# Attention of a fused layer on Trainium2: channel vectors kept as columns, one product for the maxima, and the first inverse root moved between weight pieces

## The reference

```
qkv = x @ w_qkv.T ; q, k, v = thirds of qkv            # c = 256
agent = q @ w_conv1                                    # [b, n]
agent_attn = softmax((agent * c**-0.5) @ k)            # [b, c], over channels
agent_v = softmax(v @ agent_attn)                      # [b, n], over tokens
agent_v = agent_v @ v                                  # [b, c]
agent_tok = softmax(agent[:, :, None], axis=-1)
x = layernorm(x + agent_tok * agent_v[:, None, :])
x = layernorm(x + ffn(x))        # 8 experts, 2 per token, plus a shared gated layer
```

## Time and profile before

| | |
|---|---|
| median of 3 runs | 362.53 us (361.86 to 367.12) |
| profiled execution, time | 358.51 us |
| profiled execution, span of the trace | 356.7 us |
| PE busy | 319.7 us (90%) |
| PE weight loads busy | 284.6 us (80%) |
| DVE busy | 264.1 us (74%) |
| POOL busy | 205.3 us (58%) |
| ACT busy | 191.6 us (54%) |

### The profile page before, as it was taken

The page is one execution under the profiler, slowest core; times in us unless marked ns, Lnnn a source line. Parts: engine busy times, 40 slices in busy tenths (PEclk is TensorE's granted clock), DMA queues, the critical chain, the costliest instruction groups (busy, mean ns, idle before and its releaser), DMA issues.

```text
span 356.7 us, 7798 instructions
## 1 busy us (share of the span) xinstructions
PE 319.7 (90%) x2225; PEld 284.6 (80%) x2225; DVE 264.1 (74%) x1032; ACT 191.6 (54%) x424; POOL 205.3 (58%) x241
## 2 busy tenths in 40 slices
PE   3789899899999989997987999999999989989970
PEld 1356788589788878886967999999999989978860
DVE  1876779665989898964647677676678868787786
ACT  1043777355556363734415555655655578578473
POOL 4049732736577858857273344446665855866680
PEclk9969999999999999999896999999999999999997
DMA  7967420301461212352154464446998987867953
GB/s 223 372 218 266 119 62 15 111 22 72 135 168 53 90 44 93 89 160 92 39 170 136 153 175 122 130 127 149 226 225 204 220 196 191 197 215 189 344 189 125
DMA packets 31383, 54.63 MB, mean 153 GB/s; under 512 B 4880, under 2 KB 22544, under 8 KB 31344
## 3 DMA queue, kind: packets, MB, share of 16 engines
q1 hardware_dynamic: 23136, 29.82, 27.8%
q0 software_dynamic: 8208, 24.32, 24.3%
HBM read 29.73 MB, written 24.40 MB: 152 GB/s over the span
## 4 chain that ended last, share of the span: by engine, by line
PE 44%; DVE 20%; DMA 10%; issue 8%; SPq 7%; POOL 6%; ACT 3%; another core or an unknown queue 1%; DVEq 0%; ACTq 0%; POOLq 0%
PE bank L1113 15%; PE bank L1145 8%; PE bank L996 6%; PE bank L1020 4%; PE bank L980 4%; DMA stage<-ws_t 3%; PE bank L1124 3%; PE bank L1077 3%; DVE htlo L1451 3%; DVE mix L1445 2%; POOL rows_in L582 2%; DVE xs L1242 2%; POOL w1lo L538 2%; DMA x<-rows_out 2%; DMA xs<-rows_out 2%
## 5 line engine op out<-in xcount | busy, mean ns | idle before, releaser
L640 POOL DMA_INDIRECT rows_out<-stage,place x71 | 69.3, 976 | 65.1 <-ACT stage L815 49.9
L582 POOL DMA_INDIRECT rows_in<-x,slot x64 | 64.2, 1003 | 50.3 <-DVE slot L1357 33.8
L1113 PE MATMUL bank<-w1hi,bx 128*128 x284 | 65.7, 353 | 0.9 <-DVE bx L1466 0.9
L1113 PEld LDWEIGHTS bank<-w1hi,bx 128*128 128x128 f32 x284 | 49.6, 193 | 1.5 <-issue 1.4
L815 ACT ACTIVATE stage<-bank,weight 128x256 f32<-128x256 f32 x71 | 29.8, 471 | 25.0 <-PE bank L1145 22.9
L797 ACT ACTIVATE stage<-bank 128x384 f32<-128x384 f32 (+1 forms) x36 | 17.5, 487 | 40.1 <-PE bank L1113 18.3
L1113 PE MATMUL bank<-w1lo,bx 128*128 x142 | 37.2, 342 | 2.0 <-issue 2.0
L1466 DVE TENSOR_TENSOR bx<-bank,bx 128x512 fp32r<-128x512 f32 (+1 forms) x36 | 24.4, 677 | 15.8 <-ACT bx L739 14.3
L1593 DVE TENSOR_TENSOR stage<-bank,stage 128x384 f32<-128x384 f32 (+1 forms) x36 | 19.8, 549 | 20.0 <-ACT stage L797 12.7
L1020 PE MATMUL bank<-ws2hi,hthi 128*128 128x256 f32 x96 | 28.6, 298 | 4.7 <-DVE htlo L1451 2.7
L996 PE MATMUL bank<-xthi,ws1hi 128*128 128x512 f32 x96 | 31.3, 407 | 0.0
(11 more groups left out here) (248 smaller groups left out, 868.0 us busy)
## 6 DMA issues: line engine op xcount, KB each, us to landing
stage<-rows_in SPq DMA_DIRECT2D x71, 133.0 KB
xs<-rows_out POOLq DMA_DIRECT2D x12, 512.0 KB
xs<-x SPq DMA_DIRECT2D x8, 512.0 KB, 8.2
out<-xs SPq DMA_DIRECT2D x7, 512.0 KB
stage<-w_t SPq DMA_DIRECT2D x8, 384.0 KB, 3.8
rows_in<-clear SPq DMA_DIRECT2D x16, 133.0 KB
rows_out<-stage,place POOLq DMA_INDIRECT x71
stage<-w_t SPq DMA_DIRECT2D x2, 512.0 KB, 3.9
```

The source lines that it names most:

```text
L582: pool.indirect_dma_start(rows_in[0:E * CAP, :], bass.IndirectOffsetOnAxis(slot[:, q * G + t, k:k + 1], 0), x2[q % 2][:, t, :], None).then ...
L640: pool.indirect_dma_start(rows_out[:, :], bass.IndirectOffsetOnAxis(place[:, 2 * j + b:2 * j + b + 1], 0), by[j % 4][:, b * C:(b + 1) * C] ...
L1113: mm = pe.matmul(bank_h[j % 2][:, b, 0:F], bx[j % 2][:, (2 * b + k) * P:(2 * b + k + 1) * P], w[:, bass.ds(e, 1), k, :], start=(a == 0), s ...
```

## The change

Vectors of 256 channels are kept as two columns (one for each half of 128) in place of 2 x 128 equal columns. Where PE needs one as weights it reads the column 128 times (`broadcast_to`). So the copies and scalings on DVE between the products handle 2 elements in each partition, not 256, and the first spread by DVE (`first`, 1170) is gone. The channel logits are also computed as columns, by four small products on PE; ACT exponentiates them directly into `attc`, and `token_column` and `channel_spread` are gone. The exponentials go unscaled into the token logits; the reciprocal of their sum comes in at the shift (`token_shift`, now a product of two entries of `small`) and as the scale of `value_exp`. The lane maxima go through one product with the column repeated as weights, which gives them as a row in every partition, so the second product (`token_max` on PE, 909) is gone. The warm products ahead of the maxima become 48 and 12 in place of 54, 6 and 10.

On POOL `low(3)` is cut in two halves of 768 columns with `rough_rstd(0)` between them, and `low(4)` now follows it. On ACT `token_exp(1)` stands ahead of `high(3)`, and `statistics(0)` ahead of `high(4)`.

```diff
-        DVE = ["g_row", "g", "max", "rcp", "col", "lmax", "mrow", "neg", "prcp", "s_row", "s"]
-        PE = ["g", "g_spread", "logits", "col", "r", "lmax_t", "lmax_b", "psum", "s_spread", "value"]
-        SCALAR = ["exp", "p"]
+        DVE = ["g_row", "g", "max", "rcp", "lmax", "top", "neg", "prcp", "s_row", "s"]
+        PE = ["g", "g_spread", "logits", "columns", "r", "lmax_spread", "psum", "s_spread", "value"]
+        SCALAR = ["columns", "exp", "p"]
...
             low(2)
             token_shift(1)
-            low(3)
+            low(3, 0, 2)
+            rough_rstd(0)
+            low(3, 1, 2)
             low(4)
-            rough_rstd(0)
             pool.wait_ge(s_first[1], 2)
...
             def channel_exp(b):
                 act.wait_ge(s_dve[b], dve("max"))
-                if b:
-                    act.wait_ge(s_pe[0], pe_at("col"))
+                act.wait_ge(s_pe[b], pe_at("columns"))
+                act.activation(attc[b], banks[3][:, 8:8 + 2 * KC].rearrange("p (k n) -> p k n", n=2)[:, :, 0], ACT.Exp,
+                               bias=small[:, b, 0:1]).then_inc(s_act[b], 1)
...
-                act.activation(agent[:, b, :], lv[:, b, :], ACT.Exp, bias=small[:, b, 5:6],
+                act.activation(agent[:, b, :], lv[:, b, :], ACT.Exp, bias=small[:, b, 5:6], scale=small[:, b, 1:2],
...
             value_exp(0)
+            token_exp(1)
             high(3)
-            token_exp(1)
+            statistics(0, 2)
             high(4)
-            statistics(0, 2)
             channel_exp(1)
             high(5)
...
+            def with_matrix(row, column, matrix):
+                for k in range(KC):
+                    mm = pe.matmul(row, column[:, k:k + 1].broadcast_to([P, P]), matrix[:, k, :], start=(k == 0),
+                                   stop=(k == KC - 1))
+                return mm
...
                 with_matrix(banks[4][:, 0:C], wide[b], wkt).then_inc(s_pe[b], 1)
-
-            def token_column(b):
-                pe.wait_ge(s_act[b], act_at("exp"))
-                for k in range(KC):
-                    mm = pe.matmul(banks[3][:, k * P:(k + 1) * P], att[0:1, k * P:(k + 1) * P], ones[0:1, :],
-                                   start=True, stop=True)
+                for n in range(KC):
+                    for k in range(KC):
+                        mm = pe.matmul(banks[3][:, 8 + 2 * n:10 + 2 * n], wkt[:, k, n * P:(n + 1) * P],
+                                       wide[b][:, k:k + 1].broadcast_to([P, 2]), start=(k == 0), stop=(k == KC - 1))
                 mm.then_inc(s_pe[b], 1)
...
-            warm(54, banks[1])
+            warm(48, banks[1])
             token_maxima(0)
-            warm(6, banks[1])
-            token_max(0)
-            warm(10, banks[1])
+            warm(12, banks[1])
             token_sums(0)
...
             def token_max(b):
-                vec.wait_ge(s_pe[b], pe_at("lmax_t"))
-                vec.tensor_reduce(small[0:1, b, 3:4], max_bank[b][0:1, C:C + P], AX.X, ALU.max,
-                                  negate=True).then_inc(s_dve[b], 1)
+                vec.wait_ge(s_pe[b], pe_at("lmax_spread"))
+                vec.tensor_reduce(small[:, b, 3:4], max_bank[b][:, C:C + P], AX.X, ALU.max, negate=True).then_inc(s_dve[b], 1)
             def token_shift(b):
-                vec.wait_ge(s_pe[b], pe_at("lmax_b"))
-                vec.tensor_copy(small[:, b, 5:6], max_bank[b][:, C + P:C + P + 1]).then_inc(s_dve[b], 1)
+                vec.wait_ge(s_dve[b], dve("top"))
+                vec.tensor_tensor(small[:, b, 5:6], small[:, b, 3:4], small[:, b, 1:2], ALU.mult).then_inc(s_dve[b], 1)
```

More of the change, by code:

```diff
@@ L201, in post_norm_layer @@
         prod = [mix[:, 2 + n, :] for n in range(2)]
-        first = x2[0][:, 0, 0:C]
-        wide = [x2[n][:, 1, 0:C] for n in range(B)]
-        tall = [x2[0][:, 2, 0:C], junk[:, 0, :]]
+        wide = [x2[n][:, 1, 0:KC] for n in range(B)]
+        attc = [x2[n][:, 1, KC:2 * KC] for n in range(B)]
+        tall = [x2[0][:, 2, 0:KC], junk[:, 0, 0:KC]]
         grow = [mix[:, 0, n * C:(n + 1) * C] for n in range(B)]
@@ L854, in _ @@
         def _(pe):
-            pe.wait_ge(s_wq, 32)
-            pe.wait_ge(s_a, 1)
-            for k in range(KC):
-                mm = pe.matmul(banks[0][:, 0:C], first[:, k * P:(k + 1) * P], wq[:, k, :],
-                               start=(k == 0), stop=(k == KC - 1))
-            mm.then_inc(s_apsum, 1)
+            def with_matrix(row, column, matrix):
[3 more added lines that the diff above has]
+                return mm
+            pe.wait_ge(s_wq, 32)
+            with_matrix(banks[0][:, 0:C], wcol, wq).then_inc(s_apsum, 1)
             def weighted_sum(bank, b, tiles, kind=None):
@@ L875, in rows_to_columns @@
                 for k in range(KC):
-                    mm = pe.matmul(at[:, k * P:(k + 1) * P], rows[:, k * P:(k + 1) * P], ones[:], start=True, stop=True)
-                return mm
-            def with_matrix(row, spread, matrix):
-                for k in range(KC):
-                    mm = pe.matmul(row, spread[:, k * P:(k + 1) * P], matrix[:, k, :], start=(k == 0), stop=(k == KC - 1))
+                    mm = pe.matmul(at[:, 2 * k:2 * k + 2], rows[:, k * P:(k + 1) * P], ones[:, 0:2], start=True, stop=True)
                 return mm
@@ L1167, in _, with columns @@
             vec.wait_ge(s_wq, 32)
-            vec.wait_ge(s_mem, 1)
-            for k in range(KC):
-                ins = vec.tensor_scalar(first[:, k * P:(k + 1) * P], ones[:], wcol[:, k:k + 1], None, ALU.mult)
-            ins.then_inc(s_a, 1)
+            def columns(src):
+                return src.rearrange("p (k n) -> p k n", n=2)[:, :, 0]
             def dots(row, dst, kind, b, tiles):
@@ L1197, in sums_spread @@
                 vec.wait_ge(s_pe[b], pe_at("g_spread"))
-                vec.tensor_copy(wide[b], banks[3][:, 0:C]).then_inc(s_dve[b], 1)
+                vec.tensor_copy(wide[b], columns(banks[3][:, 0:2 * KC])).then_inc(s_dve[b], 1)
             def channel_max(b):
@@ L1206, in channel_sum @@
                 vec.reciprocal(small[:, b, 1:2], small[:, b, 1:2]).then_inc(s_dve[b], 1)
-            def channel_spread(b):
-                vec.wait_ge(s_pe[b], pe_at("col"))
-                vec.wait_ge(s_dve[b], dve("rcp"))
-                vec.tensor_scalar(wide[b], banks[3][:, 0:C], small[:, b, 1:2], None, ALU.mult).then_inc(s_dve[b], 1)
             def lane_max(b):
@@ L1233, in value_spread @@
                 vec.wait_ge(s_dve[b], dve("prcp"))
-                vec.tensor_scalar(tall[b], src, small[:, b, 7:8], None, ALU.mult).then_inc(s_dve[b], 1)
+                vec.tensor_scalar(tall[b], columns(src), small[:, b, 7:8], None, ALU.mult).then_inc(s_dve[b], 1)
             def token_reciprocal(b):
@@ L1302, in _ @@
                                   ALU.add).then_inc(s_first[1], 1)
-            channel_spread(1)
             token_reciprocal(1)
@@ L1520, in group @@
                 if g == 1:
-                    value_spread(1, banks[3][:, C:2 * C])
+                    value_spread(1, banks[3][:, C:C + 2 * KC])
                 if g:
```

44 lines of the change are left out of this document (17 added, 27 removed).

## The result

The changed kernel took 368.16 us (median of 4 runs, 366.39 to 368.72), the kernel before 362.19 us beside it (361.14 to 367.12). The ratio is 1.0176, with an interval of [1.0130, 1.0222]: 6.0 us more, where 2.9 were forecast. The predicted 365.4 us was 2.8 us too low, and the range ended at 367.9. The profiled execution took 368.72 us (span 366.9).

What follows compares the result with a forecast made beforehand. It took the early wait chain over POOL's weight pieces to bound the kernel. 3.3 us lost at the held root less 0.4 gained made 2.9 us slower: median 362.53 to 365.4 us, range 360.7 to 367.9.

Steps and rivals of the forecast that it cites:

- What bounds the kernel, and the order: First 75 us: waits run over POOL's weight pieces, nearly tied with the squares; the start's gain or loss reaches the end.
- Columns and token row: Batch 0 attention: cheaper DVE steps save 2.5 us, columns cost PE 1.1; lane maxima at 25.55 instead of 27.77.
- The held shift: DVE's shift at 26.8 waits for POOL's 768-column piece, done at 28.05: 1.4 us gained, not 2.5.
- The held root: Group 0: DVE's first two root steps wait for POOL's pieces; scaling at 44.6 instead of 41.28, 3.3 us lost.
- The fixed price: Rival: each root step beside a piece takes 0.69 us whatever the piece's length; 363.5 us, chance 0.13.
- the missing hold: Rival: POOL's weight pieces do not stop the DVE steps, so the kernel gets faster; 360.8 us, chance 0.15.
- the sum: Whole kernel: 3.3 us lost at the root less 0.4 gained at group 0's end, 2.9 us slower.
- the clock: Rival: PE's clock falls in the 1.6 us gap before 28.5; 1.9 us more before the first add, 367.3, chance 0.2.
- The missed gap: Rival: DVE reaches the shift after 27.93 and waits for `low(2)` until 31.4; 6.8 us lost, 368.9, chance 0.1.
- The end of group 0: End of group 0: DVE's 0.41 us wait for the removed product goes; 0.4 us gained.

Runs made afterwards that it cites:

- e3: Kernel before with only the new order on POOL and ACT; ratio 1.0143.
- e7: Changed kernel with the old order on POOL and ACT, and the reduced maximum left in PE's memory (shift free); ratio 1.0000.
- e2: Changed kernel with the old order of POOL and ACT; ratio 1.0064.
- e9: Kernel before plus columns, maximum in PE's memory, 80 and 18 warm products, POOL's rough root after whole `low(3)`, `low(4)` behind the first scaled tiles; ratio 1.0039.
- e1: Kernel before, unchanged, run against itself; ratio 1.0002.
- e6: Changed kernel with the reduced maximum left in PE's memory, so the shift has one operand there; ratio 1.0125.
- e13: Changed kernel, unaltered, run a third time; ratio 1.0165 to the kernel before.
- e15: Changed kernel with the maximum in PE's memory and 86 and 16 warm products in place of 48 and 12; ratio 1.0143.
- e16: As e15, with 120 in place of 20 warm products ahead of the first transposes; ratio 1.0054.
- e4: Changed kernel with 86 and 38 warm products in place of 48 and 12; ratio 1.0333.
- e10: Changed kernel, unaltered, run again; ratio 1.0260 to the kernel before.
- e11: Changed kernel with maximum in PE's memory, 86 and 16 warm products, and 120 ahead of the first transposes (same kernel as e16); ratio 1.0085.
- e5: Changed kernel with 120 in place of 20 warm products ahead of the first transposes; ratio 1.0087.
- e8: Changed kernel with the intermediates of group 0's root steps in PE's memory; ratio 1.0096.

## Why the prediction was too low

- **What bounds the kernel, and the order.** Right for the loss: the first tiles' scaling carried it on, and e3 shows that the order alone costs 1.4% (0.5 to 2.4). With the old order and the shift free nothing is lost (e7, 1.0000); with the shift held it is 1.0064 (e2). "What the start gains or loses should reach the end whole" is wrong for a gain: e9's lead of 1.2 to 1.6 us was gone at the group-1 logits, for the load behind `low(4)`.
- **Columns and token row.** Right: lane maxima at 25.33 where 25.55 was forecast. Some of the match is luck of the trace compared with: e1 has them at 26.61 and not at 27.77, so the gain is 1.3 to 2.4 us. What the columns cost on PE was absorbed by the hold, as said.
- **The held shift.** Right in mechanism and, in the profile after, in size: 1.24 us, ending at 27.95. It is shown by e6 and e7, which have 0.16 us with the operand moved. But it is no fixed figure: 0.32, 1.24 and 4.78 us in three executions of the changed kernel.
- **The held root.** Right: 1.14 and 3.46 us, ended by the two pieces, and much the same (1.14 to 1.28 and 3.34 to 3.46) in every kernel with this order and the old operands. The fixed price and the missing hold fell. The Trainium skill ("SBUF — State Buffer", section "SBUF: two separate sides") has the port pair locked for a whole instruction, for two operands in SBUF and for VectorE's two-port modes. The traces agree in the first: 3.46 us for a root step with two operands in the on-chip memory, 0.17 with one. The 3.81 us of the two scalings, which have one, would fit the second, but no view shows the mode of an instruction.
- **The failing step: the sum.** "3.3 - 0.4 = 2.9" priced PE's part of the path at the clock of the kernel before. That was the rival *the clock*, with a chance of 0.2, and its 1.9 us for the sums is what the first add shows (35.44 against 33.5). It still fell short, for it looked at one gap only, and not at the right one: it feared the 1.6 us ahead of 28.5, of which 0.90 came, and the clock fell earlier, at 25.5, after the 2.27 us ahead of the lane maxima's product. The held root leaves PE idle for 5.68 us in the same way. The stretch behind it ran at the lower level and cost 2.5 us, a term that no case had. 365.4 + 1.9 + 2.5 = 369.8 against a measured 368.16. The other 1.6 us I can't place. The terms are those of one execution: in e13 the first of them is missing, and the second is 1.6 us (5.49 less 3.93). And behind group 1, where the change has little left, single executions differ by more than that: from the first product of the experts (171.41, in e1 169.49, after 176.97) to the end of the span it is 185.3 and 185.8 us in the two traces of the kernel before and 189.9 in the one after. What the times themselves show is the second term (e15 and e16); the first is shown in the traces alone.
- **The missed gap.** I gave it 0.1 on the condition that DVE came after 27.93. It happened in e4 and e10 with DVE coming at 26.69 and 27.01, inside the short piece. The condition was wrong.
- **The end of group 0.** The 0.4 us gain was in no row by itself. From the first logits to those of group 1 it was 17.4 us before and 17.0 after, which agrees with it. It goes with the new code and not with the order: 16.9 in e2, 17.3 in e3 and 17.4 in e1.

With both clock costs taken away the forecast's own sum should remain: 2.9 less about 1.1 for the shift that e16 sets free is 1.8. e16 measured 1.9 (0.6 to 3.2) and e11, the same kernel, 3.0 (1.5 to 4.5). Both allow it; that e16 meets it to 0.1 us is luck.

## What to carry to other kernels

A wait can have two prices: its own length, and the lower clock in which PE does the work behind it (here 1.0 to 2.5 us, by the execution: e4, e13 and the changed kernel; none in e9, where PE had waited 2.87 us). When a change leaves PE idle just ahead of the path, count the PE work that follows at both levels. Small DVE steps in a chain must not stand beside long POOL instructions if both operands, or input and output, are in the on-chip memory: each step can cost a whole POOL instruction. Moving one operand to PE's memory frees it, but look at the next step too; it may be held in its place. Moving the long instruction away frees all of them, but ask what waits for that one: in e9 it was a load. And profile the same kernel more than once before calling the size of a stall its price.

## What was not expected of the hardware

- A DVE step that waits inside one of two POOL instructions standing back to back is not always served between them. It was in the profile after (1.24 us, ended with the first) and in four more traces, and it was not in e4 (4.84) and e10 (4.78). When DVE came does not decide it (26.71 after, 26.69 in e4, inside the same piece); what does I don't know.
- Scaling a tile with two values per lane, 0.74 us for two tiles with POOL idle (e9), is held like a product of two arrays (3.73 and 3.81 us for two). The third root step in the earlier trace rows, 0.67 us at 91.27 with one array, had shown such a hold before.
- Whether the clock was low somewhere between 17.5 and 25 us differed between executions of one kernel (low in e13, full in the profile after). It decided whether the warm products reached the sums.
- After that, the clock dips again at 182.5 to 185.9 and at 196.2 to 199.6 us in the profile after, at 171.7 to 175.1 and 188.7 to 195.5 before. In the traces of e5 to e8, where the kernel before took 348.3 us, it does not fall between 80 and 330 us. No experiment was made on those.
